# Row maxima as the bias of four exponentials a block, in place of a product that subtracts them, in a fused tokenizer, attention and quantized feed-forward kernel

## What is computed

```python
x = jnp.einsum('bnf,df->bnd', x, W_lin) + b_lin
out = jnp.concatenate([cls, x], axis=1) + position_embeddings
...
keys = jnp.repeat(xk, N_REP, axis=2)
scores = jnp.einsum('bqhd,bkhd->bhqk', xq, keys) / math.sqrt(HD)
mask = jnp.abs(idx[:, None] - idx[None, :]) <= WINDOW // 2
scores = jnp.where(mask[None, None], scores, -jnp.inf)
attn = jax.nn.softmax(scores.astype(jnp.float32), axis=-1)
ctx = jnp.einsum('bhqk,bkhd->bqhd', attn, values).reshape(b, s, HQ * HD)
...
h = bit_linear(x, w1)              # quantized rows times ternary weights
h = depthwise_conv1d(h.transpose(0, 2, 1), conv_w, conv_b)
h = jax.nn.silu(h)
return bit_linear(h, w2)
```

## Time and profile before

| what | value |
|---|---|
| median of 3 runs | 397.09 us (396.2 to 400.3) |
| time of the profiled execution | 396.99 us |
| its span, first to last instruction | 395.2 us |
| granted TensorE clock over the span | 0.987 |
| instructions | 8402 |

### The profile page before, as it was taken

How to read it: one execution, slowest core, us unless ns; L and a number is a source line. 1 busy time by engine, 2 the same in 40 slices (tenths; PEclk the granted TensorE clock), 3 DMA queues, 4 the chain that set the end, 5 groups by cost and what they waited for, 6 DMA issues and landing times.

```text
span 395.2 us, 8402 instructions
## 1 busy us (share of the span) xinstructions
PE 364.5 (92%) x3033; PEld 273.6 (69%) x3037; DVE 301.8 (76%) x639; ACT 256.5 (65%) x483; POOL 215.0 (54%) x245
## 2 busy tenths in 40 slices
PE   6799799999999999999989999999999988987886
PEld 2376557777877886678767876788678866853743
DVE  2246649654599879888998698959895998799795
ACT  3213436568786779677868686769767966672552
POOL 5406589688479928892689427971994006001000
PEclk9889989999999999999999999999999999999999
DMA  7671521201000012002000220022011100000101
GB/s 235 166 181 41 153 99 29 54 13 28 20 19 2 2 48 50 22 21 53 19 0 2 57 48 2 2 61 44 11 27 44 27 2 13 25 2 0 35 2 35
DMA packets 21907, 16.71 MB, mean 42 GB/s; under 512 B 12435, under 2 KB 20936, under 8 KB 21865
## 3 DMA queue, kind: packets, MB, share of 16 engines
q1 hardware_dynamic: 20970, 15.11, 15.3%
q10 hardware_dynamic: 895, 1.06, 1.0%
HBM read 9.82 MB, written 3.38 MB: 33 GB/s over the span
## 4 chain that ended last, share of the span: by engine, by line
PE 65%; DVE 17%; ACT 7%; issue 5%; DMA 4%; POOL 1%; SPq 1%; DVEq 0%; ACTq 0%; POOLq 0%
PE bank L1784 8%; PE bank L1864 8%; PE bank L1835 7%; PE bank L1878 6%; PE bank L1937 5%; PE bank L1938 4%; PE bank L1907 4%; DMA shared<-in_x 4%; PE bank L1855 3%; PE bank L1731 3%; PE bank L1981 3%; DVE shared L1635 2%; PE bank L1898 2%; PE bank L1797 2%; PE bank L1847 2%
## 5 line engine op out<-in xcount | busy, mean ns | idle before, releaser
L1501 DVE TENSOR_REDUCE mx<-bank 120x4 fp32r<-120x376 f32 (+3 forms) x88 | 44.1, 506 | 26.8 <-PE bank L1847 26.2
L1273 ACT COPY pT<-bank 94x480 f32<-94x480 f32 (+3 forms) x88 | 48.1, 554 | 21.7 <-PE bank L1864 21.3
L1265 ACT ACTIVATE pr<-bank 120x376 f32<-120x376 f32 (+3 forms) x88 | 39.6, 453 | 27.1 <-PE bank L1855 26.2
L1864 PE MATMUL bank<-cst,pr 120*94 120x120 f32 (+3 forms) x352 | 51.3, 270 | 2.6 <-ACT pr L1265 2.5
L1835 PE MATMUL bank<-kbd,q_hl 128*120 128x376 f32 (+3 forms) x176 | 51.1, 374 | 1.6 <-issue 0.9
L1113 POOL TENSOR_TENSOR rs<-ve,half_neg 110x3 f32<-110x3 f32 x16 | 16.7, 1044 | 62.8 <-DVE ve L1529 47.2
L1937 PE MATMUL bank<-xT_hi,w1T 128*128 128x330 f32 x128 | 44.2, 351 | 1.3 <-DVE late L1584 0.9
L1864 PEld LDWEIGHTS bank<-cst,pr 120*94 120x94 f32 (+3 forms) x352 | 36.1, 122 | 10.0 <-ACT pr L1265 6.0
L1120 POOL TENSOR_SCALAR xn<-h,mv,rs 110x256 f32<-110x256 f32 x21 | 27.6, 1321 | 25.3 <-PE bank L1772 24.9
L1135 POOL TENSOR_TENSOR rc<-qk,cst 110x320 f32<-110x320 f32 x22 | 20.0, 908 | 38.9 <-ACT qk L1236 37.9
L1938 PE MATMUL bank<-xT_lo,w1T 128*128 128x330 f32 x128 | 39.5, 314 | 0.0
(11 more groups left out here) (131 smaller groups left out, 877.7 us busy)
## 6 DMA issues: line engine op xcount, KB each, us to landing
kbd<-shared SPq DMA_DIRECT2D x56, 41.2 KB, 2.1
out<-h SPq DMA_DIRECT2D x7, 330.0 KB
wn<-in_w SPq DMA_DIRECT2D x2, 1024.0 KB, 6.6
shared<-in_x SPq DMA_DIRECT2D x4, 432.0 KB
h<-in_txt SPq DMA_DIRECT2D x1, 770.0 KB
late<-in_lin SPq DMA_DIRECT2D x1, 768.0 KB, 7.6
vw<-v_rows SPq DMA_DIRECT2D x8, 94.0 KB
v_rows<-qk SPq DMA_DIRECT2D x8, 82.5 KB
```

Source lines behind the costliest of these rows:

```text
L1265: nc.scalar.activation(pr[:, g % 3, 0:HKV * WIDTH[j]], S_BANKS[g % 2][0:QP, 0:HKV * WIDTH[j]], ACT.Exp, scale=HD ** -0.5).then_inc(exped, 1)
L1273: nc.scalar.copy(pT[0:WIDTH[j], g % 3, :], S_BANKS[g % 2][0:WIDTH[j], 0:HKV * QP]).then_inc(p_kept, 1)
L1501: nc.vector.tensor_reduce(mx[:, g % 4, :].bitcast(F32R), S_BANKS[g % 2][0:QP, 0:HKV * WIDTH[j]].rearrange("p (k c) -> p k c", k=HKV), axis ...
L1864: o = nc.tensor.transpose(S_BANKS[g % 2][0:w, kv * QP:(kv + 1) * QP], pr[:, g % 3, kv * w:(kv + 1) * w], ident[0:QP, 0:QP])
```

## The change

The product that takes the maxima off is gone, with its table of ticks, its semaphore and its weights `neg_id` (made once by DVE, line 1395). Keys are multiplied by -1/4 where they are kept: `kvmask` holds -HD ** -0.5 for pair 0, and `keep_k` is an ACT Copy with that scale for the others. So the bank holds the negated, scaled scores, the mask adds +1e30, and the maximum is now a minimum, same shape and same bank. `exp` becomes four instructions, one for each piece, with scale -1 and the minimum of the piece's rows as its bias, a column of `mx` of 120 partitions. The semaphore that says the block is done is raised by the last of the four. The wait of DVE for a free slot of `mx`, four blocks back, is now for `exp`.

```diff
-    'pe.shift': (
-        (22, 23, 28, 34, 39, 45, 53, 56, 62, 73, 78),
...
-            c[QK * part + HD * kv:QK * part + HD * (kv + 1), C_KVM + kv] = 1.0
+            c[QK * part + HD * kv:QK * part + HD * (kv + 1), C_KVM + kv] = -HD ** -0.5
...
-        hide = np.where(seen, 0.0, NEG)
+        hide = np.where(seen, 0.0, -NEG)
...
-                    nc.scalar.copy(kT[:, part, :].bitcast(F32R), k_bank(n, part)[:, 0:T]).then_inc(k_kept, 1)
+                    nc.scalar.activation(kT[:, part, :].bitcast(F32R), k_bank(n, part)[:, 0:T], ACT.Copy,
+                                         scale=-HD ** -0.5).then_inc(k_kept, 1)
...
             def exp(n, j):
                 g = NB * n + j
-                act.wait_ge(shifted, g + 1)
+                w = WIDTH[j]
+                act.wait_ge(topped, g + 1)
                 if g >= 3:
                     act.wait_ge(p_turned, g - 2)
-                nc.scalar.activation(pr[:, g % 3, 0:HKV * WIDTH[j]], S_BANKS[g % 2][0:QP, 0:HKV * WIDTH[j]], ACT.Exp,
-                                     scale=HD ** -0.5).then_inc(exped, 1)
+                for kv in range(HKV):
+                    o = nc.scalar.activation(pr[:, g % 3, kv * w:(kv + 1) * w], S_BANKS[g % 2][0:QP, kv * w:(kv + 1) * w],
+                                             ACT.Exp, bias=mx[:, g % 4, kv:kv + 1], scale=-1.0)
+                o.then_inc(exped, 1)
...
-                    dve.wait_ge(shifted, g - 3)
-                nc.vector.tensor_reduce(mx[:, g % 4, :].bitcast(F32R),
+                    dve.wait_ge(exped, g - 3)
+                nc.vector.tensor_reduce(mx[:, g % 4, :],
                                         S_BANKS[g % 2][0:QP, 0:HKV * WIDTH[j]].rearrange("p (k c) -> p k c", k=HKV),
-                                        axis=AX.X, op=ALU.max).then_inc(maxed, 1)
+                                        axis=AX.X, op=ALU.min).then_inc(topped, 1)
...
-            def shift(n, j):
-
-                g = NB * n + j
-                w = WIDTH[j]
-                pe.wait_ge(maxed, g + 1)
-                nc.tensor.matmul(S_BANKS[g % 2][0:QP, 0:HKV * w], neg_id[:, :].bitcast(F32R),
-                                 mx[:, g % 4, :].bitcast(F32R).unsqueeze(2).to_broadcast([QP, HKV, w]),
-                                 start=False, stop=True, skip_group_check=True).then_inc(shifted, 1)
```

More of the change, by code:

```diff
@@ L191 @@
         (532, 542, 544, 551, 554, 563, 567, 571, 580, 586, 592),
-    ),
-    'pe.shift': (
[8 rows of a table removed]
     ),
@@ L833, in build @@
         identb = sb("identb", [128, 128], BF16)
-        neg_id = sb("neg_id", [QP, QP])
         ones = sb("ones", [128, 128])
@@ L943, in build @@
         warm_made = sem("warm_made")
-        identb_made, neg_made = sem("identb_made"), sem("neg_made")
+        identb_made = sem("identb_made")
         tok_summed, tok_kept = sem("tok_summed"), sem("tok_kept")
@@ L956, in build @@
         kbd_zeroed = sem("kbd_zeroed")
-        scored, maxed, shifted, exped = sem("scored"), sem("maxed"), sem("shifted"), sem("exped")
+        scored, topped, exped = sem("scored"), sem("topped"), sem("exped")
         p_turned, p_kept, ctx_done = sem("p_turned"), sem("p_kept"), sem("ctx_done")
@@ L1394, in _ @@
             nc.vector.tensor_copy(identb[:, :], ident).then_inc(identb_made, 1)
-            nc.vector.tensor_scalar(neg_id[:, :].bitcast(F32R), ident[0:QP, 0:QP], -1.0, None,
-                                    ALU.mult).then_inc(neg_made, 1)
             def sort_pix_dve(i):
@@ L1828, in scores @@
                     pe.wait_ge(identb_made, 1)
-                    pe.wait_ge(neg_made, 1)
                 if g >= 2:
@@ L1985, in _ @@
             work = {name: due("pe." + name) for name in (
-                "shift", "context", "scores", "turn_p", "turn_xn", "project", "turn_q", "turn_k", "turn_ctx", "select", "out_proj", "turn_xs", "up", "turn_max", "spread", "down", "turn_pix", "patches", "sum_w", "turn_w")}
+                "context", "scores", "turn_p", "turn_xn", "project", "turn_q", "turn_k", "turn_ctx", "select", "out_proj", "turn_xs", "up", "turn_max", "spread", "down", "turn_pix", "patches", "sum_w", "turn_w")}
             for q in TICKS:
-                for n, j in work["shift"].get(q, ()):
-                    shift(n, j)
                 for n, j in work["context"].get(q, ()):
```

## The result

The changed kernel takes 409.87 us in the median of four runs (408.8 to 411.8), the one before 397.06. The ratio is 1.031 (95% interval 1.024 to 1.039): slower by 3.1%, where 408 was forecast. The profiled execution took 408.82 us with a span of 407.0. Now and then an execution takes over 1.5% longer than the fastest of its kernel; the ratios leave such runs out, the medians do not.

What follows compares the result with a forecast made beforehand. Three engines near each other, with ScalarE's time deciding in the blocks: 272.1 us busy plus 21.3 and 16.5 idle give 309.9, 10.9 more than 299.0. On 396.99 that makes 407.9, so 408 us, range 387 to 425.

Steps and rivals of the forecast that it cites:

- TensorE stays the bound: Whole kernel: TensorE still decides, 13.4 us leave the chain and 3.2 come back, 387 us; chance 0.25.
- The piece: ScalarE's exponential: one 94-column piece costs 347 ns, four 1094 against 484, 0.61 us more a block.
- ScalarE's account: ScalarE in the 299 us stretch of blocks: 218.4 busy plus 80.6 idle, becoming 309.9 us, 10.9 more.
- the waits for the product: ScalarE's waits for the shift at 29 of 88 exponentials: 26.2 us, all taken as gone.
- The transposes' wait: ScalarE waiting for transposes in 33 places, 0.65 us each: 21.3 us, kept whole.
- The other idle time: ScalarE's remaining 33.1 us of waits for other products: half, 16.5 us, kept by choice.
- The sum: Stretch of blocks: 272.1 busy, 21.3 and 16.5 idle make 309.9 us, 10.9 more; whole kernel 407.9.
- the 22 us: TensorE's time freed by removing 88 products, at 0.25 us between starts.
- The signs: Expected in the profile after: exponential lengths and spacing, engine busy times, waits and chain shares that would show the forecast right.
- Block 36: Example block: its exponential ends 0.61 us later, and TensorE waits about 0.8 us before its transposes.
- the faster case: Whole kernel at 387 us with TensorE deciding; 29 exponentials that had waited end 0.11 us later net; chance 0.25.
- the paragraph on where the change lies: Reduction's end to exponential's end in the tightest blocks: 0.50 + 0.48 becomes 0.04 + 1.09, 0.15 us later.

Runs made afterwards that it cites:

- The added part alone: Kernel before, product kept, its exponential split into four pieces, each with a column of zeros as bias: 424.43 us, ratio 1.068.
- the fillers: Small unread products before each block's context products: three in the changed kernel 443.29 us, one 421.62; one in the one-exponential kernel 402.92.

## Why the prediction was right, and where it was only lucky

**The direction and its cause.** Shown. The added part alone costs 6.8 points, the removed part gives back 3.7, and with one exponential instead of four the same removal is a gain of 1%. The rival "TensorE stays the bound" has the sign wrong as a whole, but not its premise: time added to TensorE counts at about a half in the changed kernel, as the fillers show. There is no single bound.

**The piece.** The step put an operand at 98 ns and a joint's overlap at 98; they measured 88 and 105 (170 - 65). So four pieces are 1.03 us, not 1.09, and a block has 0.55 us more, not 0.61: 48 us instead of 53.7. The start of one piece to the next is 0.222 us in the median, where 0.249 was worked out.

**ScalarE's account.** Its total was right within 2 us and its two terms were not. Busy time was forecast as 272.1 us and is 260.0; idle as 37.8 and is 52.0. Of the 12 us too much, 5.7 are the piece. The rest is overlap, which the step left out and the traces show: beside its exponentials ScalarE's records add up to 247.7 us before and 252.8 after, but only 216.9 and 210.8 of them are busy time outside the exponentials' own. So 5.1 us of records came in beside the exponentials, but 11.2 us more of all records lie under others, and 6.1 us of busy time went. That they overlap more because ScalarE stands less is my reading; no run isolates it. Idle time was mis-sized in the step that took all 26.2 us of the waits for the product as gone: 9.3 us came back as waits for the reduction. The transposes' wait was kept at 21.3 and is 17.5. The other idle time is then some 25 us where half of 33.1 was chosen. The 408 rests on two errors of 12 and 14 us that cancel, which is luck, and the account's picture, ScalarE at 88% of the stretch, is not what the trace shows, 83%.

**How a microsecond on ScalarE turns into time.** The sum added all 53.7 us to ScalarE's account and struck 42.8 us of idle time from it, which leaves 10.9. By runs: in the kernel before 8 us cost nothing and 48 us cost 27. Without the product, from one to four pieces, ScalarE's exponentials are busy 47.4, 55.6, 60.7 and 87.5 us at ratios of 0.990, 0.998, 1.001 and 1.031 (the second without an operand): about 0.4 of a microsecond for each. The added part alone costs 27 us and the removed part gives back 14.7, so 12.4 are left. The forecast's 10.9 is near this, but by another road: its sum had no price for TensorE's time, and none for the clock, of which about 3 of the 12 us may come.

**TensorE.** 0.25 us a product rested on one pair of starts; the median of all 88 is 0.29, waits included, so the 22 us are rather low than high, and the sum does not hang on them. Its recorded busy time fell by 6.0 us in the stretch and not by about 20: the products that remain are recorded longer or stand more apart (the transposes 275 ns instead of 270, the projection 530 instead of 505), and part of the stretch was at half clock. The lengths of single products explain only a part of the difference. As a sign for a step that figure was badly chosen.

**The signs.** Exponentials of 0.33 to 0.35 us, 0.22 apart: as forecast. The waits of TensorE and its weight loads for the exponential, counted as the prediction counted its 8.5 (2.5 and 6.0), are 16.2 and 26.9, 43.1 us, where it said 15 or more: met, with a size that it did not foresee. Block 36 waits 0.86 us, forecast about 0.8. ScalarE's share of the chain 25%, forecast over 20, and TensorE's 41%, not over 60. The waits for transposes near 21: 17.5. Two figures of its rivals do not agree with its own working: the 0.11 us net of the faster case is 0.15 in the paragraph on where the change lies (the hop is left out), which would make 388 of 387, and 272.1 of 299 is 91% busy, not 90. Neither moves the forecast.

**A second source of the price.** The Trainium skill's rule ("ScalarE: Activation LUTs", "What ACT_TABLE_LOAD costs") gives about 93 ns for an operand and about 93 of overlap. The trace has 88 and 105. Its fixed part is 186 ns where these exponentials, read from PSUM, have 170; the measurement decides here. It spoke against the change, and with reason; the estimate by its figures was 57 us of added work, further off from the measured 48 than the one from rows.

**What stays open.** The clock's part is an estimate, about 3 of the 12 us, and no run isolates it. How the removal's 14.7 us divide into TensorE's time and the shorter path is not shown: a filler of like size costs 11 us with four pieces, but with one exponential 8.5, over twice what the removal gives there.

## What to carry to other kernels

Taking a product off the fullest engine by splitting an instruction of the next one into four is paid in fixed costs: here 0.065 us for each further piece and 0.088 for each bias operand, 48 us over 88 blocks of ScalarE's time for some 22 us of TensorE's. Ask first whether the split is needed: one minimum over all heads of a row keeps one instruction and made the kernel 1% faster instead of 3% slower, as long as no head's scores lie so far below another's that float32 loses them. In this kernel, with its fixed order, no engine is "the" bound. ScalarE's added time counted at nothing for 8 us in the kernel before and at about 0.4 to 0.6 in the larger steps, TensorE's added time at 0.4 to 0.55, and what was taken from an engine came back in part only.

## What the runs showed that I had not expected

Moving the transposes of 81 blocks by a single operation cost 28 us at either price of the exponential. The wait that it shortened was 16.2 us, and it lengthened another from 17.5 to 54.4: the copy behind the transposes, and the bank it frees, are tighter than the exponential ahead of them. And taking out VectorE's 88 reductions (44 us of records, 34 us of its busy time), and with them over 0.5 us of every block's path, gained nothing over the kernel with one exponential.
